# Zeroing the experts' regions in fixed pieces during attention instead of by looked-up rows at its end

## What is computed

```python
x = x + tanh(g_xattn) * xattn(layernorm(x), ctx)          # 16 heads
src = layernorm(x)
h = ln1(src + self_attention(src))                        # 16 heads
gates = softmax(h @ gW + gb); top 2 of 8 experts per row
ff = sum over the two experts of w_e * (relu(h @ W1[e] + b1[e]) @ W2[e] + b2[e])
x = x + tanh(g_ffn) * ln2(h + ff)
```

## Time and profile before

| | |
|---|---|
| median of 3 runs | 1215.42 us (1215.26 to 1216.89) |
| the profiled execution: its time, its span | 1216.49 us, 1214.7 us |
| busy: PE, DVE, ACT, POOL | 1126.1, 827.8, 688.4, 265.8 us |
| DMA packets, megabytes moved | 66597, 79.18 |
| the chain that ended last, by engine | PE 75%, issue 9%, DVE 8%, ACT 4% |

### The profile page before, as it was taken

One profiled execution on the slowest core, in us unless ns is written; L12 is line 12 of the kernel. 1 busy time (PEld: TensorE's weight loads), 2 busy tenths in 40 slices (PEclk: granted clock), 3 DMA queues, 4 the chain that ended last, 5 costly groups with the idle time before them and its releaser, 6 DMA issues.

```text
span 1214.7 us, 36448 instructions
## 1 busy us (share of the span) xinstructions
PE 1126.1 (93%) x12924; PEld 840.5 (69%) x12925; DVE 827.8 (68%) x2431; ACT 688.4 (57%) x1186; POOL 265.8 (22%) x371
## 2 busy tenths in 40 slices
PE   6999999999999999999999999999728999999964
PEld 4576766676766666676666677667517999999942
DVE  5565777776777777667777776777744666666667
ACT  4666767677666667777667776776513333333200
POOL 1011111122212111222212221222321222222233
PEclk9999999999999999999999999999968999999988
DMA  6012043222111111111111011101056222222165
GB/s 149 22 42 68 17 123 105 69 68 74 40 33 37 51 34 33 38 41 34 33 53 38 10 45 46 30 28 64 28 116 187 71 69 71 72 72 71 52 212 159
DMA packets 66597, 79.18 MB, mean 65 GB/s; under 512 B 14008, under 2 KB 52536, under 8 KB 66328
## 3 DMA queue, kind: packets, MB, share of 16 engines
q1 hardware_dynamic: 52680, 54.24, 16.2%
q0 software_dynamic: 6096, 15.66, 3.9%
q10 hardware_dynamic: 7680, 7.34, 1.9%
HBM read 51.32 MB, written 25.90 MB: 64 GB/s over the span
## 4 chain that ended last, share of the span: by engine, by line
PE 75%; issue 9%; DVE 8%; ACT 4%; POOL 1%; DMA 1%; DVEq 0%; another core or an unknown queue 0%; SPq 0%; POOLq 0%; ACTq 0%
PE quad L1299 11%; PE bank L1289 10%; PE bank L1485 9%; PE quad L1497 9%; PE quad L1311 8%; PE sums L1322 6%; PE bank L1436 4%; PE bank L1389 4%; ACT probs L777 4%; PE quad L1308 3%; PE bank L1282 3%; PE bank L1457 2%; PE bank L1322 2%; DVE row_max_C L1050 2%; DVE row_max_C L1047 2%
## 5 line engine op out<-in xcount | busy, mean ns | idle before, releaser
L777 ACT ACTIVATE probs<-quad 125x1792 f32<-125x1792 f32 (+1 forms) x128 | 213.0, 1664 | 116.9 <-PE quad L1311 116.7
L855 ACT ACTIVATE scored_half<-quad 112x750 bf16<-112x750 f32 (+1 forms) x160 | 131.4, 821 | 89.5 <-PE quad L1299 89.0
L1037 DVE TENSOR_REDUCE row_max_A<-quad 112x2 f32<-112x750 f32 x128 | 120.1, 938 | 70.0 <-PE quad L1299 66.5
L1485 PE MATMUL bank<-tile_inT,tile_w 128*128 128x128 f32 x1008 | 124.4, 277 | 0.3 <-ACT tile_w L887 0.3
L1039 DVE TENSOR_REDUCE row_max_A<-scored_half 112x2 f32<-112x750 bf16 x128 | 118.6, 927 | 3.2 <-ACT scored_half L855 1.0
L1485 PEld LDWEIGHTS bank<-tile_inT,tile_w 128*128 128x128 f32 x1008 | 119.0, 194 | 0.7 <-ACT tile_w L887 0.7
L1497 PE MATMUL quad<-output_w,hiddenT 128*128 x504 | 119.1, 380 | 0.0
L1299 PE MATMUL quad<-kT_A,qT_A 32*112 32x375 f32 x1024 | 115.2, 519 | 3.5 <-ACT probs L777 1.5
L1216 DVE TENSOR_SCALAR hiddenT<-bank,hidden_b 128x128 f32<-128x128 f32 x252 | 71.0, 344 | 63.0 <-PE bank L1485 62.6
L1289 PE MATMUL bank<-ctxT,wxk 128*128 128x375 f32 x256 | 99.1, 510 | 5.5 <-DMA bxk<-in_bxk_dram 5.5
L739 POOL DMA_INDIRECT kept_dram<-tile_out,take_back x63 | 60.4, 959 | 186.3 <-DVE tile_out L1239 179.7
(11 more groups left out here) (225 smaller groups left out, 1995.0 us busy)
## 6 DMA issues: line engine op xcount, KB each, us to landing
ctxT<-in_ctxT_dram SPq DMA_DIRECT2D x32, 375.0 KB, 3.5
tile_in<-sent_dram SPq DMA_DIRECT2D x63, 129.0 KB
join_in<-kept_dram SPq DMA_DIRECT2D x28, 256.0 KB, 3.4
hidden_w<-in_hidden_w_dram SPq DMA_DIRECT2D x8, 512.0 KB, 5.0
output_w<-in_output_w_dram SPq DMA_DIRECT2D x8, 512.0 KB, 5.7
x_in<-in_x_dram SPq DMA_DIRECT2D x32, 112.0 KB, 2.9
x_res<-in_x_dram SPq DMA_DIRECT2D x32, 112.0 KB, 3.2
kept_dram<-x_shift SPq DMA_DIRECT2D x32, 112.0 KB
```

The lines of the kernel that those rows point to most:

```text
L777: act.activation(probs[0:rows, t.buffer("probs", step), :, :], quad[0:rows, :, 0:U * T], ACT.Exp, scale=SCALE).then_inc(taken[kind_of(step ...
L855: act.activation(scored_half[:, t.buffer("half", step), 0:RT // 2 * n].rearrange("t (r s) -> t r s", s=n), quad[0:T, RT // 2:RT, 0:n], ACT ...
L1037: dve.tensor_reduce(row_max["A"][:, i:P // 2:ROWS], quad[0:T, 0:RT // 2, 0:S], AX_X, ALU.max).then_inc(taken[kind], 1)
L1485: mm = pe.matmul(hidden_bank[k][:, f * P:(f + 1) * P], tile_w[:, k, c, f * P:(f + 1) * P], tile_inT[:, k, c, :], start=c == 0, stop=c == D ...
```

## The change

A row is no longer looked up. Piece j, for j from 0 to 31, is rows 112 j to 112 j + 111 of every expert's region, piece 32 the last 128 rows; each is zeroed by two DMAs, one for each half of the 258 numbers. They are issued on SP, in turn, right behind the loads of N.load(n) and ahead of that turn's weight loads: one piece with most of the items 4 to 31, two with items 9, 15, 20, 26 and 31. The scatter of item n waits until pieces 0 to n have landed (30 and earlier), or all 33 (31). SP's block at E.rank, DVE's copy of next_row and two semaphores go. The written order of steps stays.

```diff
--- before.py
+++ after.py
@@ -46,8 +46,7 @@
 REGION = NB * T + P
 
 
-LAST_KNOWN = NB - 3
-BEHIND = (NB - 1 - LAST_KNOWN) * T + P
+FIRST_CLEAR = 4
 NT = NB * T * TOP // P + E - 1
 
 
@@ -281,7 +280,6 @@
         gate_parts = sb("gate_parts", [P, 2, DC, E])
         minus_gain, gate_shift, out_gate = (sb(n, [P, E]) for n in ("minus_gain", "gate_shift", "out_gate"))
         zero_row = sb("zero_row", [P, SENT // 2])
-        next_i = sb("next_i", [P, E], I32)
         hidden_w = sb("hidden_w", [P, DC, E * F])
         hidden_b = sb("hidden_b", [P, FC, E])
         output_w = sb("output_w", [P, FC, E * D])
@@ -407,8 +405,7 @@
         output_w_loaded = sem("output_w_loaded")
         plan_steps = sem("plan_steps")
         gate_made, row_gated, row_centred, logits_made = (sem(n) for n in ("gate_made", "row_gated", "row_centred", "logits_made"))
-        rows_known = sem("rows_known")
-        tails_zeroed = sem("tails_zeroed")
+        regions_zeroed = sem("regions_zeroed")
         xm_copied = sem("xm_copied")
         back_moved = sem("back_moved")
         spill_steps = sem("spill_steps")
@@ -557,15 +554,6 @@
                         keys_over(sp)
                         sp.dma_start(output_b[:, :], io["output_b"].rearrange("e d -> (e d)").partition_broadcast(P)
                                      ).then_inc(output_b_loaded, DMA)
-                    elif step == "E.rank" and t.item("E") == LAST_KNOWN:
-
-                        sp.wait_ge(rows_zeroed, 5)
-                        sp.wait_ge(rows_known, 1)
-                        for e in range(E):
-                            row_no = sp.value_load(next_i[0:1, e:e + 1], min_val=e * REGION, max_val=e * REGION + (LAST_KNOWN + 1) * T)
-                            sp.dma_start(io["sent"][bass.ds(row_no, BEHIND), :].rearrange("(p r) (h d) -> p (r h) d", r=4, h=2),
-                                         zero_row[0:BEHIND // 4, :].unsqueeze(1).to_broadcast([BEHIND // 4, 8, SENT // 2])
-                                         ).then_inc(tails_zeroed, DMA)
                     elif step == "F.shift":
                         n, k = t.item("F"), t.slot("F")
                         sp.wait_ge(shifted, t.item("F", 1, 1))
@@ -597,11 +585,25 @@
                         row(b, io[a]).then_inc(w_loaded["C"], DMA)
                     sp.dma_start(gate_w[:, :, :], io["gate_w"].rearrange("(c p) e -> p c e", p=P)).then_inc(w_loaded["C"], DMA)
 
+            def clear(j):
+
+                rows = T if j < NB else REGION - NB * T
+                regions = io["sent"][:, :].rearrange("(e r) d -> r e d", e=E)
+                for half in (slice(0, SENT // 2), slice(SENT // 2, SENT)):
+                    sp.dma_start(regions[j * T:j * T + rows, :, half],
+                                 zero_row[0:rows, :].unsqueeze(1).to_broadcast([rows, E, SENT // 2])).then_inc(regions_zeroed, DMA)
+
             def turn(t):
                 move(t)
                 n = t.item("N")
                 if t.only != "N.load":
                     return
+                if n == FIRST_CLEAR:
+                    sp.wait_ge(rows_zeroed, 5)
+                if n >= FIRST_CLEAR:
+                    cleared = [(NB + 1) * m // (NB - FIRST_CLEAR) for m in (n - FIRST_CLEAR, n - FIRST_CLEAR + 1)]
+                    for j in range(*cleared):
+                        clear(j)
                 for stage in ("KQV", "BC")[n] if n < 2 else ():
                     load_weights(stage)
                 if n == 6:
@@ -719,8 +721,7 @@
                         pool.wait_ge(xm_copied, t.item("E", 1, 1))
                         pool.wait_ge(row_steps, t.item("E", 6, 6))
                         settled(pool, passed_pool)
-                        if t.item("E") > LAST_KNOWN:
-                            pool.wait_ge(tails_zeroed, E * DMA)
+                        pool.wait_ge(regions_zeroed, (t.item("E") + 1 if t.item("E") < NB - 1 else NB + 1) * 2 * DMA)
                         for i in range(TOP):
                             pool.indirect_dma_start(out=io["sent"], out_offset=bass.IndirectOffsetOnAxis(
                                 ap=send_row[:, k, i:i + 1], axis=0), in_=xm[:, k, i, :], in_offset=None).then_inc(sent[k], DMA)
@@ -1106,8 +1107,6 @@
                         dve.tensor_reduce(route[:, 0:TOP], rows_pick[:, :, :], AX_X, ALU.add).then_inc(row_steps, 1)
                         dve.wait_ge(row_steps, t.item("E", 6, 5))
                         dve.tensor_copy(send_row[:, k, :], route[:, 0:TOP]).then_inc(row_steps, 1)
-                        if t.item("E") == LAST_KNOWN:
-                            dve.tensor_copy(next_i[:, :], next_row[:, :]).then_inc(rows_known, 1)
                     elif step == "F.out":
                         dve.wait_ge(made["F.out"], t.count(step))
                         dve.wait_ge(res_shifted, t.item("F", 1, 1))
```

## The result

The changed kernel takes 1229.56 us (median of four, 1226.27 to 1233.38) against 1215.58 for the kernel before: ratio 1.012, 95% interval 1.0104 to 1.0137. It is slower, by 14 us, where 7 us of gain were forecast. The profiled execution has a span of 1230.6 us against 1214.7.

A forecast was written before the change was run, and what follows sets the result against it. TensorE, busy nine tenths or more nearly throughout, was taken as the bound, except at attention's end, which waits for SP's looked-up clears. -10.6 + 3.6 = -7.0 us from 1215.42 gave 1208.4 us; eight in ten, 1204.3 to 1213.0.

The forecast's parts named there:

- The tail, -10.6 us: End of attention: without the wait for looked-up clears, the last scatter lands at 901.65 instead of 912.30, 10.6 us earlier.
- Steady passes cost nothing: Steady attention passes: x_res has 14.6 us of room, enough for two clears too, so passes stay 26.76 us.
- The price p = 4.5 us: Time a clear keeps the DMA engines, delaying what SP issues behind it: 4.5 us, range 3.3 to 7.5.
- my bounds: Cost of a clear judged from a pair of output_w loads: 3.3 us by bytes, 6.5 by pieces.
- The 37 to 45 ns a piece: Engine time per 516 B piece, from two windows of today's tails; gives 4.1 to 5.0 us for a clear's 1792 pieces.
- 640 us, 2p - 5.4: Two clears at item 26 delay the store POOL waits for; TensorE stalls at x_norm, losing 3.6 us at p 4.5.
- 72 us, p - 5.1 = 0: x_in of item 5 lands later behind a clear; loss p - 5.1, nothing at p 4.5.
- 735 us: POOL takes x_res as it lands, with free time behind it on POOL and DVE; loss p - 5.4, nothing.
- three terms: Total loss L = (2p - 5.4) + (p - 5.1) + (p - 5.4), at 640, 72 and 735 us, each not under zero.
- the slower case, queue-bound clears: Clears go no faster than today's tails, p = 7.5; TensorE stalls near 649, 78 and 744, 1218.9 us; chance 0.10.
- The far regions: Writing eight regions 3.8 MB apart might itself be slow: p 9 us, time about 1225, counted within the slower case.

The follow-up runs named there:

- second chip: The changed kernel measured again on another chip against the kernel before: 1213.60 against 1203.97 us, ratio 1.0082.
- small pieces read from DRAM: Kernel before plus 40 clears of a tensor nothing reads, 516 B pieces to eight regions, read from DRAM zeros: 1291.32 against 1204.18 us, ratio 1.0735.
- small idle pieces: Kernel before plus 40 clears in 516 B pieces to eight regions of a tensor nothing reads: 1229.92 against 1203.97 us, ratio 1.0197.
- Idle doubles: Kernel before plus 40 clears of a tensor nothing reads, two behind each x_shift store of items 5 to 24: ratios 1.0012 to 1.0735 by piece, target and source.

## Why the prediction was wrong, point by point

- **The tail, -10.6 us: right.** 10.1 by TensorE's wait for the first tile, the 0.5 being the 0.82 us rather than 0.30 between send_row and the scatter. Nothing took its place.
- **Steady passes cost nothing: right for one clear.** Passes of 26.7 us as before; x_res lands 8.1 us after issue (median), as I wrote it would. For two clears it was right behind item 20 and wrong behind item 15 on the first chip: that double cost 5.1 us, through a gap, not through x_res, the one transfer whose room I had counted.
- **The price p = 4.5 us: mis-sized on this chip.** It was to be read as half the growth of POOL's wait: (17.52 - 6.24)/2 = 5.6 us. On the second chip it is 4.3. Both lie between my bounds by bytes, 3.3, and by pieces, 6.5. The 37 to 45 ns a piece came from windows in which the engines were half busy; with the engines full, 194 to 200 us in the changed kernel, 1368 packets (some of them of hidden_w) take 6 x 16 us of engine time, 70 ns each. I took the cost of a piece from a place where the engines had room and used it where they had none.
- **640 us, 2p - 5.4: the mechanism was right, the size was not.** The room measured is 11.3 - 6.03 = 5.3 us against 5.4 forecast. With p = 5.6 the term is 5.9; the rest of the 7.5 is the lower clock behind a stall of 6 us (0.50 in the 2.7 us that follow), which I had priced at nothing.
- **72 us, p - 5.1 = 0: wrong, small.** DVE waited 5.54 us for x_in, until 75.74 where I had 73.4, so p was 6.8 there; 1.4 us lost.
- **735 us: right**, no loss in the lag.
- **What I had not seen: TensorE's own instructions travel through the same DMA engines.** The step that failed is the sentence that the price of a clear is that what SP issues behind it lands later, by p: the sum has three terms for SP's own transfers and puts the cost to TensorE's instruction packets at nothing. The page of the kernel before lists q8 with 95 packets; I read it as noise, since it takes 0.6% of the engines. Gaps and the clock behind them are 17.2 of the 26.6 us, and three quarters of the 22.9 us between the forecast for the span, -7.0, and the measured +15.9. Of the rest the double near 640 us took 3.9 more than forecast, x_in at 72 us 1.4 and the tail 0.5. None of my rivals holds it: the slower case, queue-bound clears with p = 7.5 and 1218.9 us, is the wrong mechanism and 11 us short.
- **The far regions**, which I counted within the slower case: writes to eight regions do cost more than one run in 516 B pieces (1.0197 against 1.0091), and with p at 5.6 us, not 9. The windows of 2 us in which a single clear ran in the changed kernel moved 172 to 282 GB/s. The 103 GB/s that the Trainium skill, DMA: Bandwidth & Descriptors, section on latency and other measured facts, reports for copies with rows 4 MiB apart do not show here, where the regions lie 3.8 MB apart.
- **A slip in the text:** eight tails of 352 rows are 2.9 MB, not 2.8. Nothing in the sum used it.

On instruction packets, the Trainium skill, Runtime: NRT & Kernel Launch, section on instruction fetch mechanics, says that instructions come in blocks of 16 KiB, 256 of them, over a DMA queue that the sequencer drives, and that their fetch is hidden. The packets of 16 KB and the stops every 256 records agree; that it is hidden held in the kernel before and not here, with 12.2 us of gaps. The Trainium skill, DMA: Bandwidth & Descriptors, section on queues, rings and completion order, says that an engine takes turns between its queues a packet of many descriptors at a time. No run here shows the turns, or where in them an instruction packet waits.

**What stays open.** That TensorE waits for its next block in the gaps is shown by where it stops, and that the traffic holds the block back by runs that add nothing but traffic. Why a packet starts up to 9.5 us late (11.1 with small pieces read from DRAM) was not settled, nor why the read from DRAM makes small pieces almost four times dearer. The longer pieces always came with one DMA for a clear instead of two, and no run parts the two. Why a gap comes in some doubles and not in others is the deadline in part: about one block in three of a steady pass is entered while a pair fills the engines. Whether its packet comes too late differs from pass to pass (four gaps over 2.8 us in the 20 passes with small idle pieces) and between the two profiles of the changed kernel, with and without a gap at 370 us, and that was not followed up.

## What to carry to other kernels

Before adding background DMA, ask not only what is queued behind it but what else uses the engines, and put TensorE's instruction packets on that list: cost the new traffic by its pieces at full engines, prefer few long pieces in short, even bursts. After such a change look at TensorE's waits for "issue" in the middle of runs of matmuls. Count TensorE's records up to such a wait: if the stops lie a multiple of 256 apart, it is its instructions that come late. And a forecast stall of TensorE can cost more than itself: behind 22 of the 27 gaps over 1.5 us here another 1.6 to 3.2 us of work were lost at the lower clock.

## What the runs showed of the hardware

- One instruction packet of 16 KB holds 256 records of TensorE; three come in a steady pass. In attention a packet starts 0.8 us (median, at most 5.8) after TensorE has entered the block before it in the kernel before, and up to 9.5 us after in the changed kernel. Those of the 39 gaps of 1 us and more took 1.0 to 1.9 us, and TensorE resumed 0.9 to 2.6 us after they had landed (median 1.5).
- The same 0.92 MB delays the store behind it by 4.3 us in 516 B pieces, 2.6 in 1032 B, 2.0 in 3612 B, as half of what a pair of clears adds; on another chip the first figure was 5.6.
- Idle doubles of the same bytes: ratio 1.0012 in 3612 B pieces read from DRAM, 1.0091 in 516 B pieces to one run, 1.0197 to eight regions, 1.0735 to eight regions when read from DRAM.
- Gaps of 1.34 us (one clear a pass) and 2.61 us (clears behind the stores, 413.77) left the granted clock at 1.00; behind those of 1.61, 3.59, 4.66 and 6.03 us of the changed kernel and of 3.45 us with the small idle pieces it was 0.50 to 0.59 in the 1.8 to 3.7 us that followed.
